# A re-ordered ramp: who sums the weights, which queue loads w2, and where tiles 10 and 11's statistics stand

## The reference

```python
x = x + attention(layernorm(x), ctx)   # row i may look at key j only where j % n_q == i
h = layernorm(x) * gamma + beta
xq, sx = round(h * 127/max|h|), ...    # each row; w1q = round(w1 / mean|w1|), clipped to -1..1
h = gelu(xq @ w1q.T / (sx*sw1) + b1)   # 512 -> 2048
hq = round(h * 127/max|h|)             # w2q the same way from mean|w2|
x = x + hq @ w2q.T / (sh*sw2) + b2     # 2048 -> 512
```

## Time and profile before

| | |
|---|---|
| median of 3 runs | 539.58 us (537.81 to 540.11) |
| the profiled execution | 540.51 us |
| its span, first to last instruction | 538.7 us |
| TensorE busy | 527.3 us (98%) |
| VectorE, ScalarE, GpSimd busy | 453.6, 435.9, 407.3 us |
| mean granted TensorE clock | 0.99 |

### The profile page before, as it was taken

The page is one execution under the profiler, slowest core; times in us unless marked ns, Lnnn a source line. Parts: engine busy times, 40 slices in busy tenths (PEclk is TensorE's granted clock), DMA queues, the critical chain, the costliest instruction groups (busy, mean ns, idle before and its releaser), DMA issues.

```text
span 538.7 us, 8129 instructions
## 1 busy us (share of the span) xinstructions
PE 527.3 (98%) x2434; PEld 227.4 (42%) x2434; DVE 453.6 (84%) x758; ACT 435.9 (81%) x444; POOL 407.3 (76%) x533
## 2 busy tenths in 40 slices
PE   9979989999999999999999999999999999999997
PEld 5433434444444444444444444444444444444443
DVE  3877999999989899988888887988888889887653
ACT  3558899888887888888888888888888889887762
POOL 2288687999998888888888988888888888873300
PEclk9987999999999999999999999999999999999999
DMA  8999233886565656555665556665455574535433
GB/s 310 402 387 294 69 69 102 170 208 162 135 122 141 131 148 119 129 125 130 131 143 142 123 129 117 141 132 132 124 123 130 129 142 103 92 86 100 95 78 98
DMA packets 137015, 78.72 MB, mean 146 GB/s; under 512 B 114246, under 2 KB 114310, under 8 KB 136972
## 3 DMA queue, kind: packets, MB, share of 16 engines
q1 hardware_dynamic: 135636, 75.80, 57.3%
q10 hardware_dynamic: 1335, 2.41, 1.3%
HBM read 33.88 MB, written 17.05 MB: 95 GB/s over the span
## 4 chain that ended last, share of the span: by engine, by line
PE 95%; DVE 3%; POOL 1%; ACT 1%; issue 1%; POOLq 0%; DVEq 0%; ACTq 0%
PE py L1055 41%; PE p L1040 28%; PE pab L1040 14%; PE p L983 3%; PE p L1030 3%; PE pab L1008 2%; PE pab L1030 1%; POOL xr L387 1%; PE pab L968 1%; DVE hx L792 1%; PE py L1016 1%; PE py L1008 1%; DVE w2q L779 1%; ACT hid L578 0%; PE py L974 0%
## 5 line engine op out<-in xcount | busy, mean ns | idle before, releaser
L1055 PE MATMUL py<-w2q,hqT 128*128 128x512 bf16 x1024 | 231.0, 379 | 1.7 <-DVE hqT L829 1.7
L587 ACT ACTIVATE hq<-hid,hscale 128x2048 int8<-128x2048 f32 x64 | 128.1, 2002 | 46.2 <-DVE hscale L821 46.2
L1040 PE MATMUL p<-w1q,xqT 128*128 128x512 bf16 x688 | 159.4, 380 | 0.0
L1055 PEld LDWEIGHTS py<-w2q,hqT 128*128 128x128 bf16 x1024 | 100.1, 98 | 123.0 <-DVE hqT L829 2.7
L578 ACT ACTIVATE hid<-p,xdeq 128x1024 f32<-128x1024 f32 x86 | 95.0, 1106 | 15.9 <-PE p L1040 11.2
L1040 PEld LDWEIGHTS p<-w1q,xqT 128*128 128x128 bf16 x688 | 63.8, 98 | 81.2 <-issue 10.1
L387 POOL TENSOR_TENSOR xr<-xr,attn 128x512 f32<-128x512 f32 x64 | 83.3, 1320 | 18.7 <-DVE attn L727 17.2
L402 POOL TENSOR_TENSOR hx<-hx,beta_b 128x512 f32<-128x512 f32 x64 | 91.7, 1454 | 4.4 <-ACT hx L563 4.3
L815 DVE TENSOR_REDUCE hmax<-hid 128x1 f32<-128x1025 f32 x64 | 78.1, 1220 | 18.0 <-ACT hid L578 17.4
L406 POOL TENSOR_TENSOR xr<-xr,b_b 128x512 f32<-128x512 f32 x64 | 92.6, 1465 | 0.0
L809 DVE TENSOR_REDUCE hid<-hid 128x1 f32<-128x1024 f32 x64 | 77.4, 1209 | 8.8 <-ACT hid L578 8.8
(11 more groups left out here) (88 smaller groups left out, 408.9 us busy)
## 6 DMA issues: line engine op xcount, KB each, us to landing
xr<-x SPq DMA_DIRECT2D x64, 256.0 KB, 2.9
out<-xr SPq DMA_DIRECT2D x64, 256.0 KB, 2.4
raw<-w1T SPq DMA_DIRECT2D x8, 512.0 KB, 12.2
hid<-wvT SPq DMA_DIRECT2D x8, 256.0 KB, 7.8
wout<-wout_d ACTq DMA_DIRECT2D x8, 256.0 KB, 8.7
wout<-w2T SPq DMA_DIRECT2D x3, 512.0 KB, 5.5
xr<-w2T SPq DMA_DIRECT2D x2, 512.0 KB, 11.1
attn<-ctxm_d SPq DMA_DIRECT2D x4, 256.0 KB, 8.1
```

Source lines behind the costliest of these rows:

```text
L587: nc.scalar.activation(hq8[:, t % 2, :], hid[:, t % 2, 0:HID], ACT.Copy, scale=col(hscale, t))\
L1040: mm = nc.tensor.matmul(hidden_bank(t, n), xT[:, k, :], w1q[:, k, n * D:(n + 1) * D], start=False, stop=(k == KD - 1))
L1055: mm = nc.tensor.matmul(py[:, t % 2, :], hqT[:, t % 2, c // 2, c % 2, :], w2q[:, c, :], start=(c == 0), stop=(c == 2 * NJ - 1))
```

## The change

Four kinds of edits, all in the ramp; the loops from `s = 6` on are untouched.

- w1's sum: all eight `abs_w1` on ScalarE; VectorE takes `abs_w2(0)` and `(1)` in their place, ScalarE `abs_w2(2)` to `(7)`.
- Loads: `load_w2(0)` to `(4)` are issued by ScalarE, between its own work; tile 3's rows come after w1's last pieces; the context's columns come ahead of x4; the transposes and loads behind them are re-ordered.
- TensorE: `out_rows` asks for the copies of wvo one by one; `out_rows(2)` stands behind tile 0's first layer; `weight_total(1)` between the halves of tile 1.
- The lists of VectorE, ScalarE and GpSimd are re-ordered: among much else, the last four centrings and the statistics of tiles 8 to 11 stand later on VectorE, `weight_sum(1)` ahead of `hidden_scale(0)`, and on GpSimd `scale_rows(6, 2)` and `widen_x(6, 2)` ahead of `inverse_std(10, 2)`.

The diff, cut to what is spoken of:

```diff
@@ sync @@
+            load_w1(6)
+            load_w1(7)
             load_x(3)
-            load_w1(6)
-            load_w1(7)
+            load_ctx()
+            load_b1_rows()
             load_x(4)
-            load_w2(0)
-            load_b1_rows()
             load_x(5)
-            load_w2(1)
-            load_ctx()
-            load_w2(2)
             load_x(6)
-            load_w2(3)
-            load_w2(4)
             transpose_x(0)
             load_w2(5)
             load_w2(6)
+            transpose_x(1)
             load_w2(7)
...
@@ gpsimd @@
             add_attention(1, 1)
-            add_attention(2, 1)
-            add_attention(3, 1)
             pool.wait_ge(const_set, 3)
             inverse_std(0, 1)
+            add_attention(2, 1)
             inverse_std(1, 1)
...
             inverse_std(8, 2)
-            inverse_std(10, 2)
             scale_rows(6, 2)
             widen_x(6, 2)
+            inverse_std(10, 2)
             hidden_deq(2)
             add_b2(4)
             add_attention(12, 1)
             add_beta(8, 1)
             add_beta(9, 1)
@@ scalar @@
+            abs_w1(0)
             abs_w1(1)
             copy_wvo(0)
             abs_w1(2)
             copy_wvo(1)
             abs_w1(3)
+            abs_w1(4)
             times_std(0)
             abs_w1(5)
+            times_std(1)
+            load_w2(0)
+            abs_w1(6)
+            load_w2(1)
             copy_wvo(2)
-            times_std(1)
-            abs_w1(6)
             abs_w1(7)
+            load_w2(2)
             round_x(0)
+            load_w2(3)
+            round_x(1)
+            load_w2(4)
+            round_weights(0, 1)
+            copy_wvo(3)
+            round_weights(0, 3)
...
@@ vector @@
-            abs_w1(0)
             statistics(0)
...
             centre(2)
             x_scale(0, 1)
-            centre(3)
-            statistics(4)
             weight_sum(0)
-            centre(4)
+            x_scale(1, 1)
             weight_scale(0)
+            round_w1(0)
+            clip(0, 0)
...
+            half_scale(0)
+            ctx_sum(2)
+            statistics(4)
+            weight_sum(1)
+            hidden_scale(0)
+            weight_scale(1)
...
+            x_scale(6, 2)
+            half_scale(4)
             centre(8)
             result(0)
-            half_scale(4)
             widen_h(2)
             hidden_scale(4)
+            centre(9)
+            statistics(10)
+            statistics(11)
             result(1)
+            half_scale(5)
             centre(10)
+            hidden_scale(5)
+            x_scale(8, 2)
             centre(11)
-            half_scale(5)
-            x_scale(8, 2)
-            hidden_scale(5)
             widen_h(3)
@@ tensor @@
             def out_rows(i):
-                pe.wait_ge(wvo_copied, KD)
...
                 for k in range(KD):
+                    pe.wait_ge(wvo_copied, k + 1)
...
             out_rows(0)
             out_rows(1)
             bias(0)
-            out_rows(2)
             first_layer(0, 0)
             first_layer(0, 1)
-            weight_total(1)
+            out_rows(2)
             bias(1)
             first_layer(1, 0)
+            weight_total(1)
             first_layer(1, 1)
```

More of the change, by code:

```diff
@@ L449, in _ @@
             add_beta(0, 1)
-            inverse_std(2, 2)
-            add_attention(4, 1)
             add_beta(1, 1)
-            add_attention(5, 1)
+            add_attention(3, 1)
             widen_x(0, 1)
@@ L649, in _ @@
             round_weights(1, 3)
+            gelu(2, 0)
             round_weights(1, 4)
-            gelu(2, 0)
-            times_std(6)
             gelu(2, 1)
-            round_h(1)
             round_weights(1, 5)
             round_weights(1, 6)
+            round_h(1)
+            round_x(4)
+            round_x(5)
             widen_h(0)
             round_weights(1, 7)
-            times_std(7)
             gelu(3, 0)
@@ L663, in _ @@
             widen_h(1)
+            times_std(6)
+            times_std(7)
             gelu(4, 0)
+            round_h(3)
+            gelu(4, 1)
             round_x(6)
             round_x(7)
-            gelu(4, 1)
+            widen_h(2)
             times_std(8)
-            widen_h(2)
             times_std(9)
-            round_h(3)
             gelu(5, 0)
@@ L886, in _ @@
-            attn_rows(0)
-            ctx_sum(3)
-            round_w1(0)
+            weight_sum(0)
+            x_scale(1, 1)
+            weight_scale(0)
+            round_w1(0)
+            clip(0, 0)
+            statistics(3)
+            centre(3)
+            clip(0, 1)
             round_w1(2)
-            clip(0, 0)
-            clip(0, 1)
             clip(0, 2)
             clip(0, 3)
-            attn_rows(1)
+            attn_rows(0)
+            abs_w2(0)
+            abs_w2(1)
@@ L895, in _ @@
+            ctx_sum(0)
+            x_scale(2, 2)
+            ctx_sum(1)
+            attn_rows(1)
+            half_scale(0)
[4 more added lines that the diff above has]
+            weight_scale(1)
+            centre(4)
+            ctx_sum(3)
+            statistics(5)
+            centre(5)
             attn_rows(2)
-            weight_sum(1)
+            half_scale(1)
             ctx_means()
-            weight_scale(1)
+            hidden_scale(1)
@@ L899, in _ @@
+            clip(1, 0)
+            clip(1, 1)
             x_scale(4, 2)
-            half_scale(0)
+            attn_rows(3)
             statistics(6)
             statistics(7)
-            hidden_scale(0)
-            half_scale(1)
+            clip(1, 2)
+            clip(1, 3)
+            half_scale(2)
+            hidden_scale(2)
+            clip(1, 4)
+            tail_rows_out()
+            clip(1, 5)
+            widen_h(0)
+            clip(1, 6)
+            clip(1, 7)
+            half_scale(3)
@@ L905, in _ @@
+            widen_h(1)
+            centre(6)
+            hidden_scale(3)
+            centre(7)
             statistics(8)
             statistics(9)
-            hidden_scale(1)
-            centre(6)
-            centre(7)
-            half_scale(2)
-            attn_rows(3)
-            tail_rows_out()
-            hidden_scale(2)
-            clip(1, 0)
-            clip(1, 1)
-            clip(1, 2)
-            clip(1, 3)
-            widen_h(0)
-            clip(1, 4)
-            clip(1, 5)
@@ L921, in _ @@
-            clip(1, 6)
-            clip(1, 7)
-            statistics(10)
-            centre(8)
-            statistics(11)
-            half_scale(3)
-            widen_h(1)
-            x_scale(6, 2)
-            hidden_scale(3)
-            centre(9)
+            x_scale(6, 2)
+            half_scale(4)
+            centre(8)
             result(0)
-            half_scale(4)
             widen_h(2)
             hidden_scale(4)
+            centre(9)
+            statistics(10)
+            statistics(11)
```

99 lines of the change are left out of this document (42 added, 57 removed).

## The result

The changed kernel takes 546.93 us (median of 4 runs, 546.13 to 547.76) against 539.85 us (4 runs, 537.81 to 541.34) of the kernel before: a ratio of 1.0136, interval 1.0104 to 1.0168. It is 7 us slower. The profiled execution is 546.13 us with a span of 544.3 us, 5.6 us more than the span before. The forecast was 543.2 us with a range of 535.5 to 548.0: right in its direction and within its range, but 3.7 us too low: the measured time lies 0.4 us above the range that the likeliest case had for itself.

A forecast was written before the change was run, and what follows sets the result against it. Only the ramp could change the time, through TensorE's start on tile 3's second layer: 1.3 us later plus 2.2 us of clock, 3.5 us on 540.51, gives 544.0; against the median, 543.2 us, range 535.5 to 548.

The forecast's parts named there:

- the likeliest case: Slower, because tile 3's second layer starts later and the clock drops: 541.5 to 546.5 us, chance 0.38.
- w1's sum and the first layers: Start of the ramp: TensorE's 3.50 us wait for w1's sum goes; gelu(0,0) starts at 47.8 us, 57.61 before.
- The context's columns: Ahead of out_rows(0): ctxm lands at 38.7 us, bounds 36.2 and 41.6, and TensorE waits 2.5 us.
- The rival of the queue: ScalarE's w2 loads take two thirds of the DMA rate, ctxm lands at 41.6 us: 548.9 us, chance 0.12.
- my even split: From 31.5 us ctxm and w2's loads each get half the DMA rate, so ctxm's remaining 3.6 us take 7.2.
- From w2's scale to tile 6's scale: VectorE's list of 28.4 us plus some 1.5 us of waits; x_scale(6) ends at 85.5 us, 87.87 before.
- 8 clips (4.0): In VectorE's list up to x_scale(6): eight clips take 4.0 us, from rows of 0.34 to 0.67 us each.
- Tile 0's second layer: TensorE gets tile 0's widened half at 74.4 us, 80.81 before, having waited 2.8 us.
- From tile 6's scale to tile 3's second layer: A chain through late statistics, GpSimd and VectorE takes 18.8 us, 15.2 before; the layer starts at 104.3, 1.3 us later.
- The chain through inverse_std(10) hangs on the order alone: Argument against a faster kernel: GpSimd stands 4.6 us for tile 11's statistics, with 6.5 us of work queued behind.
- The clock: TensorE stands 7 us before tile 3's second layer; half speed behind it costs 2.2 us, range 1 to 4.3.
- The rival "faster": TensorE's early lead comes through if tile 3 is widened in time: 533.5 us, middle 536, chance 0.25.

The follow-up runs named there:

- the kernel filled twice: The changed kernel with 32 unread matmuls ahead of tile 3's second layer and 22 ahead of tile 0's: 545.35 us.
- the filled kernel: The changed kernel with 32 unread matmuls in TensorE's wait ahead of tile 3's second layer: 544.92 us.
- the best kernel: The changed kernel with three order moves, b2's adds early, w2's first two sums on ScalarE, and two more moves for tile 8: 543.18 us.
- three of the kernels here: The changed kernel with three order moves, 543.51 us; also with early b2 adds and w2's first sums on ScalarE, 543.47; with two further moves, 543.18.

## Why the prediction was right, and where its sum was short

- *w1's sum and the first layers.* Right. The total at 34.16 without a wait; gelu(0,0) at 47.55 (47.8 forecast), w2's scale at 55.2 (55.6).
- *The context's columns.* 38.7 us forecast, 37.35 measured, a wait of 1.08 us in place of 2.5. The rival of the queue, which had them at 41.6, is out by its time, but its mechanism was right, and my even split was wrong. What the two queues moved from 33.5 to 37.3 us, by the DMA view of that window (q10 is ScalarE's queue, with w2; q1 SyncE's, with the columns and what follows them; packets, MB, share):

```profile
q10 hardware_dynamic: 276, 1.03, 71.7%
q1 hardware_dynamic: 280, 0.41, 30.8%
```

As many packets on either, and 71% of the bytes on the queue with the larger ones. By the rule of the Trainium skill ("DMA: Bandwidth & Descriptors", section on queues, rings and completion order) whole packets are taken in turn, and the trace agrees. That my 38.7 us came out so near was luck: w2's first packet moved only at 33.4 us, 3.9 us after its issue, where I had the sharing begin at 31.5. In other kernels with the same loads the wait was between 0 and 1.7 us, so part of it is the start's own scatter. A piece of luck is also in gelu(0,0): the columns came 1.3 us sooner than forecast, but TensorE then waited 0.74 us for tile 0's transpose, which I had as landed. It was issued at 37.66 and used at 45.22.
- *From w2's scale to tile 6's scale: the term that was too small.* 29.9 us forecast, 32.9 measured. The list was right and VectorE is busy in it almost throughout (31.48 of 32.93 us). The term that was mis-sized is "8 clips (4.0)", and with it "two widenings, ctx's sums, the attention rows and the tail (4.75 together)". I took the pitches from rows of the kernel before, where four of the clips had fallen in a pause of GpSimd (80.67, 1.43 us for four) and four beside one add and that pause (77.40, 2.75). In the new order nearly all fall beside adds, of b2 and of attention. From start to start the clips take 7.1 us, and the group of the widenings 6.5 (the widenings 2.0 of it, the scaling of 16 columns 1.1). Against this the centrings take 3.2 in place of 4.4 and the waits 0.65 in place of 1.5; the rest is within 0.3, which closes the 3.0 us. I had priced a collision for the centrings alone, where it mostly did not happen. The two kernels that take the adds of b2 away from there are 2.7 and 2.8 us faster; they touch two of the eight clips (2.15 us). The Trainium skill, "SBUF — State Buffer", section "Who interferes with whom", has this as a rule: a cast or a `tensor_scalar` in its fast mode needs the port pair that VectorE shares with GpSimd, and whoever comes second waits for the whole instruction of the other; an instruction with two inputs in SBUF contends with GpSimd's reads; a `tensor_reduce` never does. The rows agree (clips 0.75 and 2.90 us for two, centrings 0.73 and up to 1.6, the maxima of 1024 columns 1.19 to 1.22 us wherever they stand), and I had applied it to the centrings only.
- *Tile 0's second layer.* 74.4 us forecast, 76.35 measured, for the same reason, though not through the adds of b2 (without them it starts at 76.17): the wait is 5.07 us and not 2.8, and the half clock behind it is not in the forecast at all. It cost nothing there, as the kernel filled twice shows.
- *From tile 6's scale to tile 3's second layer.* 18.8 us forecast, 19.1 measured, and each link as it was put: GpSimd's stand 4.6 forecast and 4.50 measured, VectorE's 2.1 and 2.00, TensorE's 7 and 7.12. But the *reason* given was only half right. "The chain through inverse_std(10) hangs on the order alone" would mean that undoing the order gives those microseconds back, and undoing it gave 0.9 us. The waits of ScalarE behind that chain were nearly as late, so its links were the first of several; three of them undone together gave 3.4 us.
- *The clock.* 2.2 us forecast (1 to 4.3), 1.5 by the rows, up to 2.0 by the filled kernel. Right in kind; the mean granted clock is 0.70 from 107.0 to 112.3 us.
- *The sum.* 3.5 us forecast; 4.17 + 1.46 = 5.6 us in the spans and 7.1 in the medians. The 1.5 us between these two are scatter: the profiled execution of the kernel before (540.51) lay 0.7 us above its median, and that of the changed kernel (546.13) 0.8 us below its own. The loss is twice the forecast one. The time lies above the likeliest case's own range (to 546.5) and inside the stated one only by the 1.5 us that this has above it (to 548.0), so that it is inside is partly luck.

The rival "faster" failed at its condition: TensorE was 4.5 us ahead at tile 0, but VectorE not 3 us sooner at tile 6.

What stays open: how much of the loss each part of the change brings. The filled clock (2.0 us), the adds of b2 (2.8) and the order (3.4) were each shown alone, but they do not add up, and of the 7.1 us the best kernel wins back 3.8. The sums' sharing alone was tried only with a placement of my own that cost more than it told. And I can't say whether an order exists that keeps both the early sum and GpSimd's and VectorE's pace; three of the kernels here came to 543.2 to 543.5 us and stopped there, all three at tile 8's bias.

## What to carry to other kernels

In this ramp VectorE is busy nine tenths of the stretch and ScalarE and GpSimd three quarters, and removing one wait mostly moved it to the next queue. Count the work up to the event for *each* engine, and believe in a gain only if all of them get there sooner. A duration taken from a trace belongs to the neighbours it had there: when the order changes, look up for each moved VectorE instruction what GpSimd will do beside it, and price it at the collided value if that is a wide add. And a loss of clock has to be asked the same question as a wait, whether anything else is late at that point.

## What the runs showed of the hardware

Two VectorE clips of 1024 columns took 0.75 us with GpSimd idle and 2.90 us beside its wide adds, and even an instruction on 16 columns went from 0.17 to 1.20 us; the maxima next to them did not change (1.19 to 1.22 us with 1024 columns). Two DMA queues that were loaded together moved as many packets each, 276 and 280 in 3.8 us, so the one with 4 KB rows had 71% of the bytes. Behind the same wait of 5.07 us, 16 matmuls took between 5.17 and 6.43 us in different executions, where they take 3.6 at the full clock. ScalarE's DMA issues, 0.66 us each at the kernel's start, took 0.33 to 0.39 us each in the ramp and overlap its own work:

```profile
33.97 0.72 ACT L569 ACTIVATE xq<-hx,xscale 128x512 int16<-128x512 f32 x1 [0.59 <-DVE xscale L808]
33.97 0.34 ACTq L525 DMA_DIRECT2D hqT<-w2T  x1
```

The first columns of both rows are the same start: the issue ran while ScalarE rounded. And 32 unread matmuls ahead of a late operand made the kernel 2.0 us faster.
